# A perceiver kernel: half of x turned by DMA in the opening, one piece of a folded weight moved in the seam

## What is computed

```
x = x + cross_attention(layernorm(x), ctx)      # x [8,128,512], ctx [8,2048,384], 8 heads of 64
x = x + causal_attention(layernorm(x))          # one head of 512, softmax over axis 1
x = x + ffn(layernorm(x))                       # 512 -> 2048 -> 512, relu, float-quantised

# cross attention
q, k, v = x @ Wq, ctx @ Wk, ctx @ Wv
attn = softmax(einsum('bihd,bjhd->bhij', q, k) * 64**-0.5)
out  = (attn @ v).reshape(B, Nq, 512) @ Wo + bo
```

## Time and profile before

| | us |
|---|---|
| median of 3 runs | 921.82 |
| lowest, highest | 921.26, 922.07 |
| the profiled execution | 923.65 |
| its span, first to last instruction | 921.8 |
| TensorE busy | 908.5 (99%) |
| VectorE, ScalarE, GpSimd busy | 570.9, 603.8, 501.0 |
| mean granted TensorE clock | 0.998 of full |

### The profile page before, as it was taken

The page is one execution under the profiler, slowest core; times in us unless marked ns, Lnnn a source line. Parts: engine busy times, 40 slices in busy tenths (PEclk is TensorE's granted clock), DMA queues, the critical chain, the costliest instruction groups (busy, mean ns, idle before and its releaser), DMA issues.

```text
span 921.8 us, 19760 instructions
## 1 busy us (share of the span) xinstructions
PE 908.5 (99%) x7486; PEld 569.2 (62%) x7486; DVE 570.9 (62%) x1013; ACT 603.8 (66%) x1138; POOL 501.0 (54%) x391
## 2 busy tenths in 40 slices
PE   6999999999999999999999999999999999999998
PEld 4556666666666666666666666666666545544444
DVE  6756555556665555665555566555677759886634
ACT  4577777777777777777777777777766523336540
POOL 4356666556556666666655655787777764310000
PEclk9999999999999999999999999999999999999999
DMA  9347657776766787667677767967998562233502
GB/s 335 111 101 140 138 127 141 142 163 140 133 143 129 136 144 137 133 136 140 133 144 152 140 143 146 175 150 160 177 179 166 106 134 55 50 108 73 182 13 80
DMA packets 335916, 125.31 MB, mean 136 GB/s; under 512 B 311760, under 2 KB 313552, under 8 KB 335824
## 3 DMA queue, kind: packets, MB, share of 16 engines
q1 hardware_dynamic: 320880, 95.61, 54.8%
q10 hardware_dynamic: 14944, 28.45, 10.0%
HBM read 45.36 MB, written 2.10 MB: 51 GB/s over the span
## 4 chain that ended last, share of the span: by engine, by line
PE 94%; DVE 2%; DMA 1%; ACT 1%; SPq 1%; issue 1%; POOL 0%; ACTq 0%; DVEq 0%
PE v_ps L633 29%; PE k_ps L633 27%; PE e_ps L702 10%; PE e_ps L633 8%; PE o_ps L724 6%; PE o_ps L727 3%; PE e_ps L993 3%; PE o_ps L745 2%; PE o_ps L986 2%; PE e_ps L986 1%; PE v_ps L986 1%; DMA x_in<-in_x 1%; PE o_ps L926 1%; PE k_ps L986 1%; SPq L576 0%
## 5 line engine op out<-in xcount | busy, mean ns | idle before, releaser
L1913 POOL TENSOR_TENSOR p_l<-p_f,p_h 128x1024 f16<-128x1024 f32 x128 | 272.4, 2129 | 233.9 <-ACT p_f L1151 233.9
L1149 ACT ACTIVATE p_h<-e_ps,bias 128x512 f16<-128x512 f32 x256 | 175.7, 686 | 4.9 <-POOL p_l L1913 2.3
L1465 DVE TENSOR_TENSOR k_l<-k_ps,k_h 128x512 f16<-128x512 f32 x128 | 88.5, 692 | 144.9 <-ACT k_h L1123 144.9
L1151 ACT ACTIVATE p_f<-e_ps,bias 128x512 f32<-128x512 f32 x256 | 176.5, 689 | 0.0
L1457 DVE TENSOR_TENSOR v<-v_ps,v 128x512 f16<-128x512 f32 x127 | 88.1, 694 | 118.4 <-ACT v L1115 118.4
L1470 DVE TENSOR_REDUCE q_max<-e_ps 128x2 f32<-128x1024 f32 x128 | 150.9, 1219 | 9.1 <-PE e_ps L702 1.0
L633 PE MATMUL v_ps<-wv_h,ctx_h 128*128 128x256 f16 x756 | 124.3, 273 | 0.2 <-DVE v L1457 0.2
L633 PE MATMUL v_ps<-wv_l,ctx_h 128*128 128x256 f16 x756 | 123.7, 273 | 0.0
L633 PE MATMUL v_ps<-wv_h,ctx_l 128*128 128x256 f16 x756 | 123.7, 273 | 0.0
L724 PE MATMUL o_ps<-v,pt_h 128*128 128x129 f16 x1024 | 106.2, 220 | 0.4 <-issue 0.4
L1905 POOL TENSOR_TENSOR ctx_l<-raw,ctx_h 128x1536 f16<-128x1536 f32 x31 | 96.2, 3103 | 18.3 <-ACT ctx_h L1104 17.6
(11 more groups left out here) (307 smaller groups left out, 1316.4 us busy)
## 6 DMA issues: line engine op xcount, KB each, us to landing
raw<-in_ctx_t ACTq DMA_DIRECT2D x26, 768.0 KB, 5.3
w_raw<-in_w_t SPq DMA_DIRECT2D x32, 256.0 KB, 4.0
raw<-in_ctx_t SPq DMA_DIRECT2D x5, 768.0 KB, 4.7
pt_h<-p_h SPq DMA_TRANSPOSE x128, 3.4
pt_l<-p_l SPq DMA_TRANSPOSE x128, 3.2
out<-xr SPq DMA_DIRECT2D x7, 256.0 KB, 2.0
x_in<-in_x SPq DMA_DIRECT2D x6, 256.0 KB, 11.1
o_all<-in_x ACTq DMA_DIRECT2D x6, 256.0 KB, 3.6
```

The costliest lines, as they stand in the source:

```text
L1149: act.activation(p_h[:, s % H_RING, h, :], e_ps[s % 2][:, h, :], ACT.Exp, scale=EXP_SCALE, bias=bias[:, n % 2, h, q:q + 1]).then_inc(p_hi, 1)
L1151: act.activation(p_f[:, s % F_RING, h, :], e_ps[s % 2][:, h, :], ACT.Exp, scale=EXP_SCALE, bias=bias[:, n % 2, h, q:q + 1]).then_inc(p_ful ...
L1465: dve.tensor_tensor(k_l[:, n % 2, cols], k_ps[:, :], k_h[:, n % 2, cols], ALU.subtract).then_inc(k_split, 1)
L1913: pool.tensor_tensor(p_l[:, s % L_RING, :, :], p_f[:, s % F_RING, :, :], p_h[:, s % H_RING, :, :], ALU.subtract).then_inc(p_split, 1)
```

## The change

In the opening rows 4 to 7 of x are no longer turned by TensorE. ScalarE and VectorE split the normalised rows as they lie into `xn_half` (which takes the place of `wq_raw`), rows 4 and 5 behind their slot 0 and rows 6 and 7 behind slot 1, and SP turns the halves with two DMA transposes a row. The context loads 4 and 5 keep their order behind the turns. Queries 4 to 7 come in one block behind slot 4. `ctx_high(2)` moves ahead of the first `q_high`, quarter 4 is split one slot later, load 6 is issued one slot later. The waits that keep the shared buffers apart are moved into slot 0 of the softmax.

In the seam `fold(2)` comes ahead of `project_out(7)`, with the order of ScalarE and VectorE to match.

```
--- before.py
+++ after.py
@@ -100,6 +100,9 @@
     assert mybir.dt.size(F16) * (2 * DCH * B * T + 2 * DCH * D) <= p_base - ctx1_base
     assert first_end <= raw_base
 
+    x_halves, x_halves_end = place(nc, first_end - DCH * D * 4, [("xn_half", [P, 4, 2, D], F16)])
+    assert x_halves_end <= first_end
 
     late_w, late_w_end = place(nc, ctx0_base, [
         ("wo_h", [P, DCH, D], F16), ("wo_l", [P, DCH, D], F16), ("aq_h", [P, DCH, D], F16), ("aq_l", [P, DCH, D], F16),
@@ -168,6 +171,7 @@
     w_h = [late_w["aq_h"], late_w["ak_h"], late_v["av_h"], late_w["wo_h"]]
     w_l = [late_w["aq_l"], late_w["ak_l"], late_v["av_l"], late_w["wo_l"]]
     w_dram = [awq, awk, awv, xwo]
+    xn_half = x_halves["xn_half"]
     ot_h, ot_l = q_h, q_l
     o_half = waiting["o_half"]
     at_h, at_l = turned.values()
@@ -353,8 +357,8 @@
 
 
 
-        ctx_behind = {0: 2, 1: 3, 4: 4}
-        load_behind = {5: EARLY_CTX}
+        ctx_behind = {0: 2, 1: 3, 5: 4}
+        load_behind = {6: EARLY_CTX}
         for n in range(1, STAGES):
             if QUARTERS + n < B * QUARTERS:
                 ctx_behind[QUARTERS * n + 2] = QUARTERS + n
@@ -385,7 +389,12 @@
         x_groups = [range(0, 2), range(2, 4), range(4, B)]
 
 
-        QUERIES_BEHIND = {2: (4, 5), 3: (6,), 4: (7,)}
+        QUERIES_BEHIND = {4: (4, 5, 6, 7)}
+        def nt_at(what, r):
+            return 32 * (what + (1 if r >= 4 else 0))
 
 
 
@@ -528,8 +537,20 @@
                     .then_inc(small_landed, 16)
             for col, src in ((bq_col[:, :], abq), (bk_col[:, :], abk), (b1_col[:, :, 0], b1)):
                 sp.dma_start(col, src).then_inc(small_landed, 16)
-            for i in range(2, EARLY_CTX):
-                load_ctx(i)
+            def turn_x(r):
+                sp.wait_ge(xt_split, r + 1)
+                for i, half in enumerate((xt_h, xt_l)):
+                    sp.dma_start_transpose(half[:, :, r * P:r * P + P], xn_half[:, r - 4, i, :]).then_inc(nt_landed[r], 16)
+            load_ctx(2)
+            load_ctx(3)
+            turn_x(4)
+            turn_x(5)
+            load_ctx(4)
+            turn_x(6)
+            turn_x(7)
+            load_ctx(5)
 
             def turn_output(b):
                 sp.wait_ge(o_ready, PAIRS * b + PAIRS)
@@ -544,7 +565,11 @@
             for s in range(SLOTS):
                 at = s % T_RING
                 sp.wait_ge(p_hi, 2 * s + 2)
-                if s >= T_RING:
+                if s == 0:
+                    for r in range(5, B):
+                        sp.wait_ge(nt_landed[r], nt_at(0, r))
+                elif s >= T_RING:
                     sp.wait_ge(pv_done, s - T_RING + 1)
                 sp.dma_start_transpose(pt_h[:, at, :, :], p_h[:, s % H_RING, :, :].rearrange("p h j -> p (h j)"))\
                     .then_inc(pt_h_landed[at], 16)
@@ -695,7 +720,7 @@
                     pe.wait_ge(p_full, 2 * s - 2)
                 else:
                     pe.wait_ge(q_split, 4)
-                    pe.wait_ge(xt_split, B)
+                    pe.wait_ge(xt_split, 4)
                 tokens, cols = slice(b * T, b * T + T), slice(q * QW, q * QW + QW)
                 for left, right, first, last in ((q_h, k_h, True, False), (q_h, k_l, False, False), (q_l, k_h, False, True)):
                     for h, rows in enumerate(head_rows):
@@ -731,8 +756,6 @@
 
             def turn_x(r):
                 pe.wait_ge(xn_ready, r + 1)
-                if r >= 4:
-                    pe.wait_ge(xt_split, r - 3)
                 for c in range(DCH):
                     mm = pe.transpose(t_bank[r % 4][:, c * P:c * P + P], x_in[:, r, c * P:c * P + P], ident[:, :])
                 mm.then_inc(xt_filled, 1)
@@ -767,7 +790,8 @@
 
             def second_query(i):
                 pe.wait_ge(q_split, i - 1)
-                pe.wait_ge(xt_split, B)
+                for r in range(4, B):
+                    pe.wait_ge(nt_landed[r], nt_at(0, r))
                 q_part(i, 0)
                 q_part(i, 1)
                 q_part(i, 2).then_inc(q_filled, 1)
@@ -795,9 +819,6 @@
 
             for s in range(1, SLOTS):
                 steady(s)
-                if s == 1:
-                    for r in range(4, B):
-                        turn_x(r)
                 for i in QUERIES_BEHIND.get(s, ()):
                     second_query(i)
 
@@ -865,7 +886,7 @@
             def key_products(half):
                 pe.wait_ge(bias_summed, 5)
                 for r in range(4 * half, 4 * half + 4):
-                    pe.wait_ge(nt_landed[r], 32)
+                    pe.wait_ge(nt_landed[r], nt_at(1, r))
                 if half:
                     pe.wait_ge(c_summed, 2)
                 else:
@@ -934,7 +955,7 @@
                     pe.wait_ge(tr_split, 4)
                 else:
                     for r in range(4):
-                        pe.wait_ge(nt_landed[r], 64)
+                        pe.wait_ge(nt_landed[r], nt_at(2, r))
                 if j < 4:
                     pe.wait_ge(mm2_copied, len(made) - 4 + (j + 2) % 4 + 1)
                 else:
@@ -995,6 +1016,7 @@
                 mm.then_inc(y_filled, 1)
 
 
             weighted_values(SLOTS - PV_LAG)
             scores(SLOTS - 2)
             fold(0)
@@ -1009,8 +1031,8 @@
             project_out(5)
             project_out(6)
             bias_products()
+            fold(2)
             project_out(7)
-            fold(2)
             fold(3)
             project("v", 0, 0)
             for t in range(4):
@@ -1087,6 +1109,13 @@
                 act.activation(xt_h[:, :, r * P:r * P + P], t_bank[r % 4].rearrange("p (c n) -> p c n", c=DCH),
                                ACT.Copy).then_inc(xt_hi, 1)
 
+            def x_high(r):
+                act.wait_ge(xn_ready, r + 1)
+                if r == 4:
+                    act.wait_ge(wq_split, DCH)
+                act.activation(xn_half[:, r - 4, 0, :], x_in[:, r, :], ACT.Copy).then_inc(xt_hi, 1)
             def q_high(i):
                 half, p = i // 4, i % 4
                 act.wait_ge(q_filled, i + 1)
@@ -1142,6 +1171,9 @@
 
                 n, q = stage_of(s)
                 act.wait_ge(bias_ready, s + 1)
+                if s == 0:
+                    act.wait_ge(xt_split, B)
                 if s >= H_RING:
                     act.wait_ge(pt_h_landed[(s - H_RING) % T_RING], 16 * ((s - H_RING) // T_RING) + 16)
                 if s >= F_RING:
@@ -1163,6 +1195,7 @@
             k_high(0)
             wk_high(slice(P, D))
             ctx_high(1)
+            ctx_high(2)
             for i in range(3):
                 q_high(i)
             wv_high(1)
@@ -1208,12 +1241,12 @@
             for s in range(SLOTS):
                 n, q = stage_of(s)
                 steady(s)
-                if s == 1:
-                    for r in range(4, B):
-                        turned_high_x(r)
+                if s < 2:
+                    x_high(4 + 2 * s)
+                    x_high(5 + 2 * s)
                 for i in QUERIES_BEHIND.get(s, ()):
                     q_high(i)
-                if s in ctx_behind:
+                if s in ctx_behind and s:
                     ctx_high(ctx_behind[s])
                 if s in load_behind:
                     load_ctx(load_behind[s])
@@ -1288,7 +1321,7 @@
                 act.wait_ge(t_step, 3 * k + 3)
                 if k == 0 and u == 0:
                     for r in range(B):
-                        act.wait_ge(nt_landed[r], 64 if r < 4 else 32)
+                        act.wait_ge(nt_landed[r], nt_at(2 if r < 4 else 1, r))
                 act.activation(t_half[:, k, 0, u, :].rearrange("p (a n) -> p a n", a=2), token_unit(k, u), ACT.Copy)\
                     .then_inc(t_hi, 1)
 
@@ -1325,8 +1358,8 @@
             act.wait_ge(small_landed, 96)
             norm_high(1, 6)
             fold_high(2)
+            fold_high(3)
             norm_high(1, 7)
-            fold_high(3)
             for t in range(4):
                 z_high(0, t)
             for name in WEIGHTS[:2]:
@@ -1445,6 +1478,11 @@
                 dve.tensor_tensor(xt_l[:, :, rows], t_bank[r % 4].rearrange("p (c n) -> p c n", c=DCH),
                                   xt_h[:, :, rows], ALU.subtract).then_inc(xt_split, 1)
 
+            def x_low(r):
+                dve.wait_ge(xt_hi, r + 1)
+                dve.tensor_tensor(xn_half[:, r - 4, 1, :], x_in[:, r, :], xn_half[:, r - 4, 0, :], ALU.subtract)\
+                    .then_inc(xt_split, 1)
             def q_low(i):
                 half, p = i // 4, i % 4
                 cols = slice(half * 512, half * 512 + 512)
@@ -1554,9 +1592,10 @@
 
             for s in range(SLOTS):
                 steady(s)
+                if s < 2:
+                    x_low(4 + 2 * s)
+                    x_low(5 + 2 * s)
                 if s == 1:
-                    for r in range(4, B):
-                        turned_low_x(r)
                     wk_low(1)
                 elif s == 2:
                     wv_low(1)
```

(8 more changed lines are left out.)

4 lines of the change are left out of this document (1 added, 3 removed).

## The result

| | before | after |
|---|---|---|
| median of 22 runs each, us | 921.63 | 922.76 |
| lowest, highest | 920.41, 925.46 | 921.67, 924.66 |
| ratio, 95% interval | | 1.0014 [1.0008, 1.0021] |
| the profiled execution | 923.65 | 922.43 |
| its span | 921.8 | 920.6 |

I forecast 920.9, between 918.8 and 922.0. The two profiled executions alone say the opposite of the medians: after is 1.22 us faster there, where I had forecast 0.9. That contradiction is what the experiments had to settle.

A forecast was written before the change was run, and what follows sets the result against it. TensorE, busy 99% of the span, was taken to bound the kernel. The opening's +2.4 us and the seam's -3.3 summed to -0.9, from the median 921.8 to 920.9 us, range 918.8 to 922.0.

The forecast's parts named there:

- the one from the profiled execution to the median: Whole run: the -0.9 us worked out on the profiled span of 921.8 was applied to the median, giving 920.9.
- The seam term of the sum: At project_out(7): fold(2) ahead of it saves 1.58 us of wait and 1.70 of lower clock, 3.28 us.
- The seam itself: No wait ahead of project_out(7), clock 1.00 throughout 746 to 756, "v" projection 3.3 us nearer to the bias products.
- first wait: At values(3): 2.36 us of stall for v_low(2), behind row_norm under ctx_low(2), then x_low(4) and x_low(5).
- Second wait: At values(4): 0.4 us of stall for v_low(3), with x_low(7) standing under ctx_low(3).
- Third wait: At values(5): 1.6 us of stall for v_low(4), which hangs on the first softmax step.
- Sum of the opening: The opening: -1.98 us removed, stalls of 2.36, 0.4 and 1.6 uncovered, together +2.4 us.
- The clock's fall in the opening: Rival: TensorE's stands at 31.7 and 43.8 lower the clock; one fall costs 1.7 us, 922.6, two 924.3; chance 0.08.
- The fall in the seam: Rival: the clock still falls behind the thin bias products, 1.7 us of gain missing, 922.6; chance 0.06.
- The light opening: Rival: the opening costs only 0.3 to 1.5 us, time 918.8 up to 920.1; chance 0.30.

The follow-up runs named there:

- look_before: The kernel before, unchanged, profiled once more; 921.02 us.
- e1: The kernel before with the seam's part of the change alone; median 921.42 us, ratio 0.9990.
- e3: The changed kernel with all x_low on VectorE behind slot 1; median 922.00 us, ratio 1.0002.
- e4: The changed kernel with ctx_high(2) put back behind slot 0; median 923.52 us, ratio 1.0021.
- e9: The changed kernel with wv_low(1) alone moved from behind slot 2 to behind slot 4; median 922.79 us, ratio 1.0014.
- e2: The changed kernel with the seam's old order put back, so the opening's part alone; median 923.02 us, ratio 1.0018.
- e5: The changed kernel with slot 1's value and key halves ahead of all x_high and x_low, wv_low(1) behind slot 4; median 920.14 us, ratio 0.9979.
- e7: The changed kernel with the turn of the last head outputs made late, behind the four w1 loads; 927.64 us.
- e8: e5 with q_low(3) and v_low(2) ahead of the four row_norm on VectorE; median 920.25 us, ratio 0.9986.
- e6: The kernel before with the turn of the last head outputs made late, behind the four w1 loads; 929.10 us.

## Why the prediction was wrong

**The step that failed is the one from the profiled execution to the median.** I wrote that it "is 1.8 above the median of the runs; the difference goes onto the median". The 3.28 us of the seam, 1.58 of wait and 1.70 of clock, were real in that execution: after has won them back there (13.03 to 9.59 us, 3.44). But they were also why that execution was slow. The other profiled execution of before has neither [look_before], and by time and clock (921.02 us, 1.000) it is like most, 27 of 35. In such an execution there is nothing to gain, and e1 measures just that: 921.42 against 921.42. The gain can exist at most in the 8 runs of 35 with a fall, and where in the run the clock fell in these is not on record. Both warnings stood in the profile: an execution above every one of the three timed runs, and a mean clock of 0.998, which the earlier trace rows alone explain. The seam term of the sum, -3.3, was 0 for the median; in the mean it is at most some 0.8 (8 of 35 times 3.4, an estimate). That the forecast missed by only 1.9 us is in part luck: the opening, taken at +2.4, was priced 0.8 too dear (below), and that error went the other way.

**The seam itself** went as drawn in the profiles of after and e1: no wait, clock up throughout, the "v" projection earlier, logits(0) without a new gap.

**The opening, first wait.** Forecast 2.36 us at values(3), measured 2.31; row_norm under ctx_low(2) and x_low ahead of v_low(2) as worked out, the end of v_low(2) 0.3 us later (34.20 against 33.9). The 2.31 is counted from the end of the last matmul. My 2.36 was counted between starts, and so counted it is 2.47: after 31.22 the next matmul was due at 31.87 (before, the same step is 31.06 to 31.71), and values(3) started at 34.34.

**Second wait.** Forecast 0.4, measured none. I had x_low(7) stand under ctx_low(3). ctx_low(3) waited instead. VectorE went from one such instruction to the next without letting GpSimd in (x_low, x_low, wk_low, to 36.46). In e3 GpSimd got in between x_low(7) and wk_low(1), and the wait came. The Trainium skill ("SBUF — State Buffer", section "SBUF: two separate sides") speaks of an exclusive lock, held for a whole instruction; the rows of e3, e4 and after agree that it is one, and in none of them do two such instructions run side by side at their own pace. Which side gets it next I could not derive.

**Third wait.** Forecast 1.6, measured 0.93 (1.09 between starts): smaller, since with no x_low(7) held up k_low(2) and q_max(0) came 0.6 to 0.7 us earlier (q_max(0) at 40.55, forecast 41.25). Its cause, wv_low(1) ahead of q_max(0), is shown by e9, where moving it takes the wait away.

**Sum of the opening.** Forecast +2.4; by its own terms, counted between starts, -1.98 + 2.47 + 1.09 = +1.58. The profiles agree: values(8) starts at 71.24 in after and at 69.66 in look_before. So the opening was 0.8 us dearer in the forecast than in the trace: 0.4 from the second wait and 0.5 from the third, less 0.1 from the first. To this comes 0.53 us that I had not foreseen, in the FFN, where TensorE now waits for a turned tile. TensorE's row of after, then SP's rows of after and of look_before for the turns ahead of it:

```profile
839.42 0.59 PE L1007 MATMUL k_ps<-tt_h,ws_h 128*128 128x512 f16 x2 [0.53 <-DMA tt_l<-t_half]
```
```profile
825.02 2.39 SPq L624 DMA_TRANSPOSE tt_h<-t_half  x1
```
```profile
825.53 1.26 SPq L599 DMA_TRANSPOSE tt_h<-t_half  x1
```

The third of these turns holds the queue for 2.39 us in place of 1.26, and so in e2 and e5, the same wait with it; in e3, e4, e7, e8 and e9 the four take 0.6 to 0.8 us longer than before and TensorE does not wait for them. None of before, look_before, e1 and e6 shows it. The list of DMA queues names what lies on the long turn, a small load of instructions on queue 8. First after between 825 and 826 us, then look_before between 820 and 821, ahead of its four turns (the first at 821.46):

```profile
q8 instruction: 1, 0.02, 7.8%
```
```profile
q8 instruction: 1, 0.02, 6.9%
```

In all eight profiles of kernels with the new opening one of the four turns is long (the third in after, e2 and e5, the fourth in e3, e4, e7 and e8, the second in e9), and this load starts within it, in e3 0.2 us ahead of it. In the four without, it starts 1.2 to 1.4 us ahead of the first turn. All kernels with a long turn issue eight more turns on SP in the opening; if the load is one of SP's own instructions, which no row says, these would move the place where it falls. No run moved the load by itself, so this cause is argued and not shown.

**The balance of two executions without a fall**, look_before to after: +0.79 us at the first bias product (+1.58, less 0.5 us, since look_before has 0.9 us of issue gaps in all and after 0.4, and less 0.3 that I did not trace), -0.06 in the seam, +0.53 in the FFN, 0.1 elsewhere; spans 919.2 and 920.6, +1.4. The medians without falls are 1.2 apart by the 35 runs of before, 921.13 to 922.36. In the 22 runs of before measured beside after, whose clocks are not on record, those under 924 us have 921.5, which makes it 0.8. The balance of one pair of executions is thus no closer than about half a microsecond.

**The rivals.** The clock's fall in the opening, to which I gave 0.08, happened, as far as can be told, in 8 runs of 22 (the place is seen in the profiles of e2, e7 and e9, not in these runs) and costs 1.54 us between the group medians, near the 1.7 that I had taken. I argued that dense work ahead of the stand would prevent it; e2 shows it after dense work. Nor did the fall of the earlier trace rows come while TensorE did nothing, as I had written: TensorE worked again from 748.10, and the granted clock is still 1.00 in 748.25 to 748.50 and 0.62 in the quarter of a microsecond behind it. The fall in the seam happened in no run of e1, and in e7 only with a turn made late. The light opening did not come in full: row_norm lay under ctx_low(2), and only the second wait and part of the third were lighter. All in all runs with a fall became more frequent: 13 of 76 of before, 21 of 45 of the three kernels that keep the long first wait (after 8 of 22, e2 6 of 12, e9 7 of 11).

## What to carry to other kernels

Before pricing a wait from one profiled execution, ask whether that execution is a typical one: if its time lies above the timed runs and its clock below theirs, the gaps in it may be what makes it slow, and their removal moves the tail of the distribution, not its middle. A second profile of the unchanged kernel would have settled it here. And when work is taken off the engine that bounds, list what ran beside it: the transposes and queries that left slots 1 and 2 had covered waiting for VectorE, 3.2 us of which came to light, and the order of the instructions on VectorE and ScalarE, not their amount, decided how much (922.76 us for after, 920.14 for e5 with the same instructions).

## What the runs showed that I had not expected

- The DMA turn of q_l, a 128x512 f16 tile, took 2.5 us from issue to landing in nine of ten profiled executions and 4.2 in one (before), with the same loads issued 1.3 us behind it; in e6 and e7, with four 256 KB loads issued just ahead, the turns of q_h and q_l took 5.3 to 6.4. What decides between 2.5 and 4.2 wasn't found.
- TensorE standing 1.0 us in the opening never cost the clock (e5, 0 of 12 runs), nor did 1.70 and 1.37 us (e4, 0 of 12); standing 2.2 to 2.3 us did in 21 runs of 45 (after, e2, e9). The lengths are those of one profiled execution each.
- Of VectorE and GpSimd either can be the one that waits while the other reads: VectorE for 2.9 us (wk_low(1), 3.45 in place of 0.55) and 4.6 (two x_low, 5.90 in place of 1.28), GpSimd for 1.2 (ctx_low(3), 4.27 in place of 3.11).
- A turn on SP took 2.39 us in place of 1.26 where a load of instructions came beside it, and TensorE waited 0.53 us for the turned tile, 780 us later than the change in the opening.
